# A graph attention kernel: node front and first group rearranged, edge transfers moved to ScalarE's queue

## The reference, cut to what matters

```python
h = relu(layernorm(x)) @ W_node.T            # 4 heads of 32
e = edge_attr @ W_edge.T
att = sum(concat(h[src], h[dst], e) * a)     # a score for each edge and head
att = where(att > 0, att, 0.2 * att)
m = max(segment_max(att, dst), 0)
ex = exp(att - m[dst])
denom = segment_sum(ex, dst) + (n_edges - deg) * exp(-m)
out = x + segment_sum(ex / denom[dst] * h[src], dst)
```

## Time and profile before

| | before |
|---|---|
| median of 3 runs | 2135.16 us |
| profiled execution, own time | 2140.84 us |
| its span, first to last instruction | 2139.10 us |
| mean granted TensorE clock | 0.735 |
| PE busy | 1062.3 us (50%) |
| DVE busy | 1453.3 us (68%) |
| ACT busy | 546.2 us (26%) |
| POOL busy | 1534.8 us (72%) |
| read from and written to HBM | 116 GB/s over the span |

### The profile page before, as it was taken

How to read it: one execution, slowest core, us unless ns; L and a number is a source line. 1 busy time by engine, 2 the same in 40 slices (tenths; PEclk the granted TensorE clock), 3 DMA queues, 4 the chain that set the end, 5 groups by cost and what they waited for, 6 DMA issues and landing times. The chain is left out here.

```text
span 2139.1 us, 30479 instructions
## 1 busy us (share of the span) xinstructions
PE 1062.3 (50%) x7173; PEld 850.9 (40%) x7173; DVE 1453.3 (68%) x3430; ACT 546.2 (26%) x586; POOL 1534.8 (72%) x1631
## 2 busy tenths in 40 slices
PE   5564555445455553554545555454555555345441
PEld 5412444334334442444434434343444444334331
DVE  8725676576576764676757667575767667676768
ACT  4423313113122231231322313122232313131302
POOL 6577777777777777777777777777777777777730
PEclk9877877677677876776777777777777776666676
DMA  6576666556566565565656656565666666555544
GB/s 204 144 239 172 186 172 171 158 165 170 157 170 172 163 186 149 157 196 150 191 157 174 172 157 196 157 191 161 182 169 175 173 178 174 134 154 138 154 127 155
DMA packets 333783, 360.99 MB, mean 169 GB/s; under 512 B 57757, under 2 KB 290109, under 8 KB 320679
## 3 DMA queue, kind: packets, MB, share of 16 engines
q1 hardware_dynamic: 274935, 196.81, 29.6%
q0 software_dynamic: 50304, 107.57, 22.2%
q10 hardware_dynamic: 8368, 54.66, 7.7%
HBM read 229.63 MB, written 18.57 MB: 116 GB/s over the span
## 5 line engine op out<-in xcount | busy, mean ns | idle before, releaser
L153 POOL DMA_INDIRECT gath<-node_table,src_i x1563 | 1489.4, 953 | 499.2 <-issue 484.9
L963 PE MATMUL bank<-vals,onehot 128*128 128x137 f32 x1992 | 400.8, 351 | 35.4 <-DVE acc L1248 35.4
L963 PEld LDWEIGHTS bank<-vals,onehot 128*128 128x128 f32 x1992 | 391.6, 257 | 51.1 <-DVE acc L1248 41.9
L960 PE MATMUL bank<-block_1h,zero_b 128*128 128x411 bf16 x311 | 137.4, 442 | 543.6 <-DVE acc L1248 298.2
L1120 DVE TENSOR_TENSOR zs<-gath,te 128x128 f32<-128x128 f32 x52 | 19.7, 379 | 468.0 <-DMA gath<-gath 467.9
L1041 ACT ACTIVATE bank<-arg 128x128 f32<-128x128 f32 x52 | 14.6, 281 | 1164.4 <-DVE arg L1195 1164.4
L963 PE MATMUL ps_oht<-vals,onehot 128*128 128x137 f32 x1328 | 269.3, 353 | 20.4 <-DVE acc L1248 20.4
L963 PEld LDWEIGHTS ps_oht<-vals,onehot 128*128 128x128 f32 x1328 | 263.5, 259 | 30.9 <-DVE acc L1248 24.5
L960 PE MATMUL ps_oht<-block_1h,zero_b 128*128 128x411 bf16 x208 | 92.7, 446 | 366.4 <-DVE acc L1248 207.2
L960 PEld LDWEIGHTS bank<-block_1h,zero_b 128*128 128x128 bf16 x311 | 35.1, 113 | 578.6 <-issue 297.4
L1035 ACT ACTIVATE onehot_t<-onehot_t,pcol 128x4096 bf16<-128x4096 bf16 x52 | 192.8, 3709 | 255.0 <-DMA onehot_t<-key_rows 249.3
(11 more groups left out here) (212 smaller groups left out, 1140.0 us busy)
## 6 DMA issues: line engine op xcount, KB each, us to landing
gath<-gath SPq DMA_DIRECT2D x1664, 66.0 KB
onehot_t<-key_rows ACTq DMA_DIRECT2D x52, 1024.0 KB
eattr<-edge_attr_in SPq DMA_DIRECT2D x46, 1024.0 KB
gath<-node_table,src_i POOLq DMA_INDIRECT x1563
node_table<-onehot SPq DMA_DIRECT2D x14, 462.0 KB, 4.1
gath<-x_in SPq DMA_DIRECT2D x14, 448.0 KB, 4.7
edge_scores<-edge_out SPq DMA_DIRECT2D x49, 64.0 KB
gath<-edge_attr_in SPq DMA_DIRECT2D x3, 1024.0 KB, 7.0
```

What stands on the lines that cost most here:

```text
L153: nc.gpsimd.indirect_dma_start(out=ring[:, t % RING, :], out_offset=None, in_=table, in_offset=bass.IndirectOffsetOnAxis(ap=src_i[:, t:t + ...
L960: T.matmul(into[:, 0:SPAN * ACC], zero_b[:, :], block_1h[:, 0:SPAN * ACC], start=True, stop=False)
L963: last = T.matmul(at, onehot[:, a, j, :], vals[:, a, j, :], start=not wide, stop=j == BATCHES[b][-1])
```

## The change

- Front, VectorE: no slot matrices in iterations 0 to 3; four in iteration 11, five in 12, four in 13; `keep_tgt` comes before them.
- Front, ScalarE: `bytes_of` comes behind the last evacuation.
- Front, SyncE: the last group's rows are stored in three parts, each as soon as it is copied out.
- Front, POOL: FRONT = 32, the whole ring is gathered in the first block.
- Edge tiles 1, 2, 3 and 5 get homes of their own (tile 1 in the third half, 2 and 5 in the first half of `onehot`, 3 in its second half), so `copies(2)` waits for two edge scores. Edge tiles 2 and 3, the flags, the edge stores and the loads back are issued by ScalarE; SyncE keeps edge loads 4, 5 and 6 in `start` and otherwise only copies from the ring.
- The first two groups' `compare_keys` become one VectorE comparison each. `turn_edges(0)` stands behind all six first edge scores. ScalarE runs one exponential of 128x1 in `start`.

```diff
-        FRONT = 2 * BLK
+        FRONT = RING
+        in_halves = gath_flat[:, third:third + 16 * P]
+        in_onehot = [oh_flat[:, q * 16 * P:(q + 1) * 16 * P] for q in range(2)]
+        EATTR_HOME = {1: (in_halves, s_ea[1], 1), 2: (in_onehot[0], s_ea[2], 1), 3: (in_onehot[1], s_ea[3], 1), 5: (in_onehot[0], s_ea[2], 2)}
...
+                    def store_last(g):
+                        for n, (b0, b1) in enumerate(((0, 3), (3, 6), (6, W))):
+                            if n < 2:
+                                sp.wait_ge(s_thirds, n + 1)
+                            else:
+                                sp.wait_ge(n_["rows"], g + 1)
+                            sp.dma_start(tab_g[g, :, b0:b1, :], rows[:, g % 2, b0:b1, 0:ROW]).then_inc(s_rows[g % 2], 16)
...
-                    at = {0: [0], 1: [1], 2: [2], 3: [3]}
-                    at.update({N_NODE_GROUPS - 3 + n: range(4 + 3 * n, 7 + 3 * n) for n in range(3)})
+                    at = {N_NODE_GROUPS - 3: range(0, 4), N_NODE_GROUPS - 2: range(4, 9), N_NODE_GROUPS - 1: range(9, TB)}
...
+                        if g:
+                            keep_tgt(g - 1)
                         for k in at.get(g, ()):
                             slot_matrix(k)
...
-                        if g:
-                            keep_tgt(g - 1)
...
-                        if g == N_NODE_GROUPS - 3:
-                            bytes_of(dst_lo, dst_hi, 1)
                     evacuate(N_NODE_GROUPS - 1)
+                    bytes_of(dst_lo, dst_hi, 1)
...
                         elif h == 2:
-                            sp.wait_ge(s["edge_ps"], AHEAD)
+                            sp.wait_ge(s["edge_ps"], 2)
...
                     def load_edges(t):
-                        sp.wait_ge(s["edge_ps"], t - 1 if t <= AHEAD else t)
+                        sp.wait_ge(s["edge_ps"], {4: 1, 5: 3, 6: 5}[t])
...
                     def start(g):
-                        for t in range(AHEAD):
-                            if t < 4:
-                                copies(t // 2, [t % 2])
-                            if t + 2 <= AHEAD:
-                                load_edges(t + 2)
-                            store_edges(t)
-                            if t + 1 == CG:
-                                load_edge_rows(0)
-                                load_flags(g)
+                        copies(0, [0])
+                        load_edges(4)
+                        copies(0, [1])
+                        load_edges(5)
+                        copies(1)
                         copies(2)
+                        load_edges(6)

                     def body(g, prev, nxt, second):
-                        if nxt:
-                            load_flags(g + 1)
-                        if (g.n + 2) % CG == 0 and (g.n + 2) // CG < NCH:
-                            load_edge_rows((g.n + 2) // CG)
-                        t = g.n + AHEAD
-                        if t + 1 < NTG:
-                            load_edges(t + 1)
-                        if t < NTG:
-                            store_edges(t)
...
-                        pe.wait_ge(s["edge_out"], min(CG * c + AHEAD - 1, NTG) if c else AHEAD - 2)
+                        pe.wait_ge(s["edge_out"], min(CG * c + AHEAD - 1, NTG) if c else AHEAD)
...
+                    def scores_to_dram(t):
+                        edge_scores_out(t)
+                        if AHEAD <= t < NTG - 1:
+                            load_edges(t + 1)
+                        act.wait_ge(s["edge_out"], t + 1)
+                        act.dma_start(edge_rows_of(t), edge_out[:, t % 2, :].rearrange("p (i e) -> p i e", e=P)).then_inc(s_er[t % 2], 16)
...
                     def start(g):
                         load_keys(g)
+                        for t in range(2, CG):
+                            load_edges(t)
+                        load_flags(g)
                         cast_sel(0)
+                        S.activation(alpha[:, 0:1], pcol[:, 0:1], ACT.Exp, scale=0.0)
                         for t in range(2):
-                            edge_scores_out(t)
+                            scores_to_dram(t)
                         targets_out(g)
...
                         exponentials(g)
                         rescale_factor(g)
+                        if nxt:
+                            load_flags(g + 1)
                         if (g.n + 2) % CG == 0 and (g.n + 2) // CG < NCH:
+                            load_edge_rows((g.n + 2) // CG)
                             cast_sel((g.n + 2) // CG)
                         if second:
                             load_keys(g + 2)
                         if g.n + AHEAD < NTG:
-                            edge_scores_out(g.n + AHEAD)
+                            scores_to_dram(g.n + AHEAD)
...
+                    def compare_keys(g):
+                        dve.wait_ge(s_kl, 16 * (g.n + 1))
+                        V.tensor_scalar(onehot_t[:, :, :], onehot_t[:, :, :], pcol[:, 0:1], None, ALU.is_equal).then_inc(s["oht"], 1)
```

More of the change, by code:

```diff
@@ L277, in _ @@
                             load(g + XBUF + 1)
-                        store(g)
+                        if g + 1 < N_NODE_GROUPS:
+                            store(g)
+                        else:
+                            store_last(g)
                     for t in range(2):
@@ L285, in _ @@
                     for q in range(2):
-                        sp.wait_ge(s_rows[q], 16 * (N_NODE_GROUPS // 2))
+                        sp.wait_ge(s_rows[q], 16 * ROW_STORES[q])
                     sp.wait_ge(s_flags_out, 16)
@@ L527, in evacuate @@
                             act.wait_ge(n_["tgt"], g - 1)
-                        S.copy(rows[:, q, 0:3, :], v3(h_bank[0], WP))
-                        S.copy(rows[:, q, 3:6, :], v3(h_bank[1], WP))
+                        first = S.copy(rows[:, q, 0:3, :], v3(h_bank[0], WP))
+                        second = S.copy(rows[:, q, 3:6, :], v3(h_bank[1], WP))
                         S.copy(rows[:, q, 6, :], h_bank[2]).then_inc(n_["rows"], 1)
+                        if g + 1 == N_NODE_GROUPS:
+                            first.then_inc(s_thirds, 1)
+                            second.then_inc(s_thirds, 1)
                     def weights():
@@ L1061, in start @@
-                        compare_keys(g)
+                        for t in range(2, CG + 1):
+                            scores_to_dram(t)
+                        load_edge_rows(0)
+                        scores_to_dram(CG + 1)
                         turned_out(0)
                         load_keys(g + 1)
-                        for t in range(AHEAD - 2, AHEAD):
-                            edge_scores_out(t)
                         targets_out(g + 1)
-                        compare_keys(g + 1)
@@ L1098, in make_onehot @@
                             dve.wait_ge(s["iota"], 1)
+                            dve.wait_ge(s["edge_ps"], AHEAD)
                         V.tensor_tensor(onehot[:, a, :, :], ps_iota.unsqueeze(1).broadcast_to((P, GS, P)),
@@ L1256, in start @@
                         key_flags(g)
+                        compare_keys(g)
                         dve.wait_ge(s_keys_stored, 16)
@@ L1274, in body @@
                             adds(g + -1, 1, range(2, 4))
+                        else:
+                            compare_keys(g + 1)
                         weighted_rows(g, 0)
```

54 lines of the change are left out of this document (27 added, 27 removed).

## The result

The kernel after takes 2158.61 us, the median of 6 runs (2153.59 to 2170.84); the kernel before, run beside it, takes 2134.37 (6 runs, 2131.33 to 2137.25). The ratio is 1.0124, with an interval of 1.0097 to 1.0150: slower by 24 us where no change was forecast, and 18 us above the upper end of the range.

A forecast was written before the change was run, and what follows sets the result against it. POOL, making gathers one after another every 1.25 us, was taken as the bound. The terms -3.1-3.1-1.8-2.9+1.0+12.3-2.3-0.4 sum to -0.3, so 2135.16 became 2134.9 us, range 2130.8 to 2140.8.

The forecast's parts named there:

- Front, groups 0 to 3: VectorE's first four iterations lose their slot matrices: -3.1 us, bounds -1.0 (x loads become the bound) and -3.7.
- Front bound by DMA: Rival: groups 0 to 3 give only 1.0 and the store in thirds 0.7; 2138.1 us, chance 0.15, inside no change.
- Front, last groups: ScalarE's byte casts go behind the last evacuation, so the last row copy ends earlier: -3.1 us, bounds -1.5 and -3.3.
- Thirds: The front's last store, sent in three parts, lets POOL start sooner after the last row copy: -1.8 us, bounds -0.7 and -2.3.
- 32 gathers ahead: First block: the gap after 16 gathers goes, -2.9 us; more overlap with VectorE costs +1.0, bounds 0 and +3.
- The new stop: Before gather 32, POOL waits on a full ring until the first 8 are copied: +12.3 us, bounds +10.8 and +18.
- the first rival: ScalarE's three 1 MB transfers hold the first batch of copies: 6.9 instead of 0.5 us, 2141.3; chance of slower 0.2.
- The old stop: Before gather 64: the 2.60 us gap shrinks because copies(2) waits for two edge scores, not six: -2.3 us.
- The rival of the edges too far: copies(3) comes 10 us later than counted, and each further us costs one; counted in the slower chance, 0.2.
- The tail: At the end, the flag load before the last copies leaves SyncE's path: -0.4 us.
- Steady groups: Each group's flag load, edge load and edge store move to ScalarE, hidden by its 22 us wait per group: no cost.
- all bounds good: Rival, faster: matrices 3.7, hand-overs 3.3, thirds 2.3, no added overlap, stop 10.8; -4.8 us, 2130.4, chance 0.15.

The follow-up runs named there:

- x6: The kernel before with one edit: edge loads of tiles 7 to 48 issued by ScalarE directly behind the load of the keys; 2149.83 us, ratio 1.0077.
- y4: The kernel before with the three front edits alone (slot matrices late, byte casts late, last store in thirds), FRONT = 16; 2134.33 us, ratio 0.9985.
- z2: The changed kernel with ScalarE loading edge tiles 2 and 3 in start behind the first and second edge scores; 2166.63 us in a single execution.
- y1: The changed kernel with the edge loads of tiles 7 to 48 back on SyncE, at the head of each group's body; 2148.63 us, ratio 1.0050.
- y2: The changed kernel with the steady edge loads still issued by ScalarE, but later, behind compare_keys; 2147.50 us, ratio 1.0047.
- y3: The changed kernel with FRONT = 16 again instead of 32; 2153.40 us, ratio 1.0076.

## Why the prediction was wrong

The mechanism of the front and of the full ring was right, one rival was the truth in part, and the step that failed was one priced at nothing: the edge loads on ScalarE's queue in the steady groups.

**Front, groups 0 to 3.** Forecast -3.1, by taking 0.6 off for x. The first four iterations gave 3.7, the upper bound, and no x load was waited for on the way; the wait of the earlier trace rows and a smaller one (0.17) were that execution's own, since x6, with the same front, has neither. At project(11) the gain against the shown trace is 4.9, of which 1.1 are those x waits. "Front bound by DMA" did not happen in after; y4, with the same front, has two such waits (0.35 and 0.54).

**Front, last groups.** Forecast -3.1; 12.35 us from project(11) to the last copy's end became 9.21, -3.1. But part of the 12.35 was again that execution's: x6 takes 10.89. So the arithmetic was right against the trace shown, and against a usual execution this is worth 1.7. **Thirds.** Forecast -1.8, measured -0.7, the lower bound: the time from the last copy to the first gather is still 5.3 us.

**32 gathers ahead.** The block's gap went, as forecast, and the overlap with VectorE cost 1.5 where +1.0 stood: 44.5 us would have brought gather 32. The Trainium skill ("SBUF — State Buffer", Who interferes with whom) gives tensor_tensor no two-port mode, but says more than the prediction took from it: with both inputs in SBUF it contends with GpSimd's reads. No run here takes single instructions of VectorE away, so whose the 1.5 are stays open.

**The new stop.** Forecast 12.6, measured 17.38. Last gather to first copy took 4.05, not 3.40. From the first copy to gather 32 it took 13.33, not 9.2, and z2 shows the cause: 5.4 us for two transfers of 1 MB, which I had priced at 0.5. This was the first rival, given a chance of 0.2, with 6.9 as its full price; it said that it decides from 4.6 us beyond the 0.5, and 4.9 came. Its counter-argument, "batch 0 had one such transfer in front already and took only 1 us more", read an issue time (6.12 against 5.09), while what counts is the landing. The Trainium skill ("DMA: Bandwidth & Descriptors", Queues, rings and completion order) has an engine take turns between queues, packet by packet, from which I worked out some 3 us for the copies. The trace agrees with the turns (136 packets against 125 in the late window), but not with the half: equal turns are equal times only where packets are alike, and here they are 8 KB and 528 bytes. So the measured 5.4 lies nearer to the whole of the added transfers, whose 2 MB take 6.0 us at the 350 GB/s of that window.

**The old stop.** Forecast -2.3, and no gap stood before gather 64. The first weighted rows came 50.5 us after the first copy, at the end of my 45 to 50, and gather 80 did not wait. The rival of the edges too far did not happen in after; y1 shows what it looks like (3.44 before gather 80). **The tail** gave -0.4, as forecast.

**Steady groups: the step that failed.** It stood in the text as "ScalarE gets a flag load, an edge load and an edge store in each group, 0.35 to 0.6 each" with ScalarE's 22 us of waiting as cover. That prices the issue on the issuing engine, which indeed costs nothing. It left out what the moved transfer does to the others on the way: an edge tile that stood behind the critical copies now runs beside them, right behind the keys. x6 prices this one move at +16 us; undone or put off it gives back 8.9 and 9.6 in the groups (y1, y2). That is most of the +11.0 that the groups cost against y4's. The forecast had even the sentence for it, in the first rival, but looked for it only in the first batch, and 42 edge loads were moved.

It rested on a second reading: "SyncE waits 156 us for gathers to land", so SyncE has slack. The 156 us are a sum over the run. Late in it a group needs fewer gathers, and the slack shrinks: in before, SyncE waits 41.8 us for gathers from 400 to 760 us, some 4.4 a group, but 19.5 from 1400 to 1740, some 2.1 a group. Three us more of landing in each group is more than that; the group goes from 36.9 us to 37.9 in x6 and 38.1 in after, and POOL stands 3 to 5 us once in three groups. A window of the waits late in the run would have told.

**The size of the whole.** The rival's 2141.3 was still 17 us short of 2158.61. Of the 23.7 between 2134.9 and 2158.61, by the ledger, 4.8 us are the stop, 11.0 the groups (against y4's), 1.8 the front (against x6's), 0.5 the overlap, 0.7 the old stop, which was worth 1.6 and not 2.3, and 5.0 the distance from after's profiled execution to its median, which no trace explains. The ledger says where time lies, not what each part is worth alone: y3 has no stop, and its groups took 11.0 longer. The sum of the rival "all bounds good" was wrong as well: its own terms give -4.1, 2131.1, not -4.8, 2130.4.

## What to carry to other kernels

A DMA that is moved to another engine's queue has two prices: its issue, which an idle engine hides, and its bytes, which it now sends beside transfers that it used to stand behind. In these traces two busy queues passed about as many packets each, so small rows lost to large ones. Before moving one, look at what is in flight when it will be issued, and whether somebody waits for that to land; a queue's own order may be what protected it, and a later moment may do as well. Slack is to be read where it is least, from a window late in a loop whose work per pass varies, and the profiled execution's own waits are to be checked against the median before they are counted as gain.

## What was not expected of the hardware

- After eight copies of 66 KB, 0.5 MB in all, the next batch could start 4.35 us after the last issue with one 1 MB transfer beside them on the other queue, and 7.96 and 8.36 us after it with two (x6 and after, beside before). The DMA engines were 92% busy and moved 322 GB/s in after's wait.
- While both queues had work they passed about as many packets (114 and 115, 136 and 125), and so 0.93 MB of keys beside 0.05 MB of copies, and 1.00 MB of edges beside 0.06.
- The mean over 170 to 2050 us shows nothing of it: the DMA share is 0.60 before and 0.59 after, with 168 GB/s in both.
- On one chip some of SyncE's batches of copies took over twice as long to issue (11.9 us in the one shown), and every kernel took some 3000 us, before too. An experiment there measures another bound.
- An early start can be worth nothing: in the traces, y3 was 10.9 us ahead of after at gather 64 and started its last gather within 0.03 us of it.
